# Six layers of local attention and feed-forward: feed-forward loads spread over the queue, inverse roots refined on GpSimd, and new orders within a slot

## What is computed

```python
def attn_layer(x, Wqkv, qs, ksc, Wo):            # 16 heads of 64 channels
    q, k, v = jnp.split(x @ Wqkv, 3, -1)         # x is 128 wide, q, k, v 1024 each
    q = l2norm(q) * qs
    k = l2norm(k) * ksc
    q = q * cos * scale + rotate_half(q) * sin * scale
    k = k * cos * inv + rotate_half(k) * sin * inv
    out = local_attention(q, k, v)               # windows of 32 that see 64 keys
    return out @ Wo
def ffn_layer(x, g, bln, W1, b1, W2, b2):
    xn = (x - mu) / jnp.sqrt(var + 1e-05) * g + bln
    a, gate = jnp.split(xn @ W1 + b1, 2, -1)     # 341 each
    return a * jax.nn.gelu(gate, approximate=False) @ W2 + b2
for i in range(6):
    x = attn_layer(shift_tokens(x), ...) + x
    x = ffn_layer(shift_tokens(x), ...) + x
```

## Time and profile before

| | us |
|---|---|
| median of 3 runs | 3313.07 |
| range of them | 3311.14 to 3315.81 |
| time of the profiled execution | 3313.3 |
| its span | 3311.3 |
| mean granted clock of PE, as a share of 2.4 GHz | 0.977 |

### The profile page before, as it was taken

One profiled execution on the slowest core, in us unless ns is written; L12 is line 12 of the kernel. 1 busy time (PEld: TensorE's weight loads), 2 busy tenths in 40 slices (PEclk: granted clock), 3 DMA queues, 4 the chain that ended last, 5 costly groups with the idle time before them and its releaser, 6 DMA issues.

```text
span 3311.3 us, 181592 instructions
## 1 busy us (share of the span) xinstructions
PE 3127.5 (94%) x71268; PEld 2192.9 (66%) x71268; DVE 2909.5 (88%) x6045; ACT 2666.0 (81%) x5440; POOL 2449.6 (74%) x2672
## 2 busy tenths in 40 slices
PE   6777899999999999999999999999999999999997
PEld 4443567676676767667676677777677776667665
DVE  7886789999899999899999899999899999899995
ACT  6886678888788888788888788888788888788884
POOL 3333678787788878778787787878788887788883
PEclk9887899999999999999999999999999999999997
DMA  2000112122221212212122222222221222212122
GB/s 78 8 7 9 47 51 59 50 59 70 63 59 50 59 50 80 63 51 58 51 58 71 66 55 53 56 53 83 57 56 53 56 53 82 59 51 58 51 53 55
DMA packets 150136, 182.22 MB, mean 55 GB/s; under 512 B 51334, under 2 KB 73924, under 8 KB 149316
## 3 DMA queue, kind: packets, MB, share of 16 engines
q1 hardware_dynamic: 150084, 181.53, 20.5%
HBM read 21.32 MB, written 2.10 MB: 7 GB/s over the span
## 4 chain that ended last, share of the span: by engine, by line
PE 84%; DVE 5%; issue 5%; ACT 2%; DMA 1%; POOL 1%; SPq 1%; DVEq 0%; ACTq 0%; POOLq 0%
PE bank L1221 20%; PE bank L1332 10%; PE bank L1231 9%; PE bank L1308 9%; PE bank L1291 7%; PE bank L1259 7%; PE bank L1361 4%; PE bank L1239 4%; PE bank L1320 4%; PE bank L1369 4%; PE bank L1283 2%; PE bank L1352 2%; PE bank L1346 1%; DMA zm<-zm 1%; DVE XP L833 1%
## 5 line engine op out<-in xcount | busy, mean ns | idle before, releaser
L493 POOL TENSOR_TENSOR qk<-ta,tb 128x512 f32<-128x512 f32 x768 | 971.5, 1276 | 3.7 <-DVE tb L935 3.7
L1221 PE MATMUL bank<-wqkv,zsT 128*128 128x512 f32 x1536 | 821.6, 617 | 13.0 <-ACT vt L674 10.3
L502 POOL TENSOR_TENSOR qk<-qk,rn 128x512 f32<-128x512 f32 x768 | 778.0, 1045 | 4.8 <-DVE rn L954 4.8
L932 DVE TENSOR_TENSOR ta<-bank,rot 128x512 f32<-128x512 f32 x768 | 526.7, 686 | 69.7 <-ACT sq L657 34.5
L935 DVE TENSOR_TENSOR tb<-bank,rot 128x512 f32<-128x512 f32 x768 | 522.2, 680 | 0.0
L533 POOL TENSOR_TENSOR P<-P,rowsum 128x512 f32<-128x512 f32 x384 | 393.0, 1045 | 154.3 <-DVE rowsum L1052 154.3
L657 ACT ACTIVATE sq<-bank 128x512 f32<-128x512 f32 x768 | 465.1, 606 | 14.9 <-PE bank L1221 12.7
L1037 DVE TENSOR_REDUCE bank<-sq 128x32 f32<-128x2048 f32 x192 | 440.6, 2295 | 25.1
L508 POOL TENSOR_TENSOR rstd<-ve,half_neg 128x1 f32<-128x1 f32 x192 | 105.8, 551 | 474.8 <-DVE ve L992 474.8
L665 ACT ACTIVATE qkT<-bank 128x512 f32<-128x512 f32 x768 | 396.6, 602 | 63.0 <-PE bank L1259 63.0
L712 ACT ACTIVATE znT<-bank,gb 128x128 f32<-128x128 f32 x192 | 87.8, 458 | 445.4 <-PE bank L1352 445.4
(11 more groups left out here) (130 smaller groups left out, 5750.4 us busy)
## 6 DMA issues: line engine op xcount, KB each, us to landing
vs<-vt SPq DMA_DIRECT2D x1152, 128.0 KB, 2.4
wqkv<-L_ffn_Wqkv SPq DMA_DIRECT2D x6, 1024.0 KB, 5.1
zm<-zm SPq DMA_DIRECT2D x192, 31.8 KB
wqkv<-L_ffn_Wqkv SPq DMA_DIRECT2D x6, 512.0 KB, 3.8
wo<-L_ffn_Wo SPq DMA_DIRECT2D x6, 512.0 KB, 4.0
z_sb<-x SPq DMA_DIRECT2D x4, 512.0 KB, 5.7
ctxb<-ctx SPq DMA_DIRECT2D x32, 64.0 KB, 1.8
w<-L_ffn_W SPq DMA_DIRECT2D x6, 341.0 KB, 3.0
```

The lines of the kernel that those rows point to most:

```text
L493: g.tensor_tensor(o, i0, i1, ALU.add).then_inc(s["g_add"], 1)
L502: g.tensor_tensor(q3, q3, r3, ALU.mult).then_inc(s["g_qk"], 1)
L932: v_.tensor_tensor(ta[:, c].rearrange("p (h d) -> p h d", d=DH), bank[j % 2][:, :].rearrange("p (h d) -> p h d", d=DH), rot[:, o:o + 64].u ...
L1221: t_.matmul(bank[j % 2][:, :], zsT[:, pu, :], wqkv[:, 512 * j:512 * j + 512], start=True, stop=True).then_inc(s["p_qk"], 1)
```

## The change

Six things change. (1) `load_ffn` is split. The layers' g, b and b1 are loaded once at the start into small_all, and each layer copies its own 128x8 numbers into the tile small with one DMA inside the chip; W1, W2 (now 2 DMAs), b2 and this copy are spread over SP's list around the last and first shifts of two layers. (2) The clamped sums of squares go to a buffer ssq in SBUF, and the refining of the inverse root moves from VectorE to GpSimd, as four instructions of 128x32 (`refine`); the factor 0.5 goes into the rotation tables. (3) The sums of exponentials go to a buffer esum in SBUF. (4) With that, `transpose_qk` waits for d_clamp in place of d_rn and no more for d_rec. (5) PE does `proj_qk(3)` ahead of `transpose_P`, and `ffn_a` ahead of `proj_qk(0)`. (6) VectorE, ScalarE and GpSimd get new orders within the slot.

```diff
+            def load_small(layer):
+                wait(sp, "a_gelu", B * layer)
+                wait(sp, "d_h", B * layer)
+                sp.wait_ge(s["l_small"], 128)
+                sp.dma_start(small[:, :], small_all[:, layer, :]).then_inc(s["l_gb"], 16)
...
+                        sp.dma_start(small_all[0:m, :, 2 + 3 * h + c:3 + 3 * h + c],
+                                     b1[:, h * FF + o:h * FF + o + m].rearrange("l (p o) -> p l o", o=1),
...
             load_o(0)
-            load_ffn(0)
+            load_b2(0)
+            load_w1(0)
+            load_w2(0)
+            load_all_small()
+            load_small(0)
             for b in range(2, B):
                 sp.wait_ge(s["x_A1"], b - 1)
...
+                shift_z(start, 0)
+                if layer > 0:
+                    load_small(layer)
+                    load_w2(layer)
+                shift_v(start + 3, 1)
...
                 if layer + 1 < DEPTH:
+                    load_b2(layer + 1)
                     shift_v(end + 2, 0)
-                    load_ffn(layer + 1)
+                    load_w1(layer + 1)
...
+                def refine():
+                    if m_on:
+                        y = rn[:, pm, :]
+                        wait(pool, "a_rn", count(1, m, 1))
+                        wait(pool, "d_clamp", count(1, m, 1))
+                        g.tensor_tensor(nr[:, 0, :], ssq[:, pm, :], y, ALU.mult).then_inc(s["g_nr"], 1)
+                        wait(pool, "g_nr", count(3, m, 1))
+                        g.tensor_tensor(nr[:, 1, :], nr[:, 0, :], y, ALU.mult).then_inc(s["g_nr"], 1)
+                        wait(pool, "g_nr", count(3, m, 2))
+                        g.tensor_tensor(nr[:, 2, :], three[:, :], nr[:, 1, :], ALU.subtract).then_inc(s["g_nr"], 1)
+                        wait(pool, "g_nr", count(3, m, 3))
+                        g.tensor_tensor(y, nr[:, 2, :], y, ALU.mult).then_inc(s["g_rn"], 1)
...
@@ VectorE's slot @@
                 sum_squares()
-                root(0)
+                clamp()
                 gated()
                 sum_rows()
-                root(1)
+                invert()
                 z_mid()
-                root(2)
-                invert()
-                root(3)
                 rotary(0)
+                rotary(1)
                 z_out()
-                rotary(1)
+                rotary(2)
                 norm_stats()
                 norm_aggr()
-                rotary(2)
                 norm_var()
                 rotary(3)
...
@@ ScalarE's slot @@
+                copy_v(1)
+                square(0)
                 log_sum()
-                copy_v(1)
+                square(1)
                 inverse_root()
-                square(0)
-                if d_on and not (isinstance(n, int) and n - 3 >= UNITS):
-                    act.preload_act_table_set("gelu_and_others")
-                square(1)
                 copy_T(0)
                 copy_T(1)
                 copy_T(2)
+                square(2)
                 copy_T(3)
-                square(2)
+                square(3)
                 copy_PT(0)
-                square(3)
                 copy_PT(1)
                 copy_z()
+                if d_on and not (isinstance(n, int) and n - 3 >= UNITS):
+                    act.preload_act_table_set("gelu_and_others")
                 copy_zn()
...
@@ transpose_qk on PE @@
-                        wait(pe, "d_rn", count(1, m, 1))
+                        wait(pe, "d_clamp", count(1, m, 1))
                         wait(pe, "d_sub", count(2, b - 1, 2))
-                        wait(pe, "d_rec", count(1, b - 1, 1))
```

More of the change, by code:

```diff
@@ L106, in build @@
         w2 = sb("w2", [128, 3, E])
-        gb = sb("gb", [128, 2])
-        b1c = sb("b1c", [128, 6])
+        small_all = sb("small_all", [128, DEPTH, 8])
+        small = sb("small", [128, 8])
         b2r = sb("b2r", [128, E])
@@ L121, in build @@
         rn = sb("rn", [128, 2, 2 * HEADS])
+        ssq = sb("ssq", [128, 2, 2 * HEADS])
+        nr = sb("nr", [128, 3, 2 * HEADS])
+        three = sb("three", [128, 2 * HEADS])
+        esum = sb("esum", [128, HEADS])
         half_neg = sb("half_neg", [128, 2 * HEADS])
@@ L305, in load_o, with load_all_small @@
                 sp.dma_start(wo[:, :, :], Wo[layer, :, :].rearrange("(i p) n -> p i n", p=128)).then_inc(s["l_wo"], 16)
[L307 to L311, removed]
+            def load_all_small():
+                sp.wait_ge(s["u_small"], 1)
                 for o, src in ((0, lng), (1, lnb)):
-                    sp.dma_start(gb[:, o:o + 1], src[layer, :].rearrange("(p o) -> p o", o=1)).then_inc(s["l_gb"], 16)
+                    sp.dma_start(small_all[:, :, o:o + 1], src.rearrange("l (p o) -> p l o", o=1),
+                                 allow_slow_non_contiguous=True).then_inc(s["l_small"], 16)
@@ new lines, in load_w1, with load_w2, load_b2 @@
+            def load_w1(layer):
+                wait(sp, "p_a", B * layer)
+                sp.dma_start(w1[:, :], W1[layer, :, :]).then_inc(s["l_w1"], 16)
+            def load_w2(layer):
+                wait(sp, "p_y2", B * layer)
+                sp.dma_start(w2[:, 0:2, :], W2[layer, 0:256, :].rearrange("(c p) n -> p c n", p=128))\
+                    .then_inc(s["l_w2"], 16)
+                sp.dma_start(w2[0:FF - 256, 2, :], W2[layer, 256:FF, :]).then_inc(s["l_w2"], 16)
+            def load_b2(layer):
+                wait(sp, "g_zmb", B * layer)
@@ L538, in slot @@
                 add(3)
+                residual()
+                add(0)
+                refine()
                 norm_rstd()
+                add(1)
+                next_input()
                 normalize(0)
                 normalize(1)
+                add(2)
                 normalize(2)
                 normalize(3)
[L544 to L548, removed]
             slots(pool, slot, xslot)
@@ L1034, in sum_squares, with clamp @@
                         wait(dve, "a_sq", count(4, m, 4))
-                        wait(dve, "d_rn", count(1, m - 1, 1))
+                        wait(dve, "d_clamp", count(1, m - 1, 1))
                         wait(dve, "d_sub", count(2, c, 2))
-                        v_.tensor_reduce(sm, sq[:, :].rearrange("p (h d) -> p h d", d=DH), AX.X, ALU.add)\
+                        v_.tensor_reduce(SC[0][:, 0:32], sq[:, :].rearrange("p (h d) -> p h d", d=DH), AX.X, ALU.add)\
                             .then_inc(s["d_sumsq"], 1)
+                def clamp():
+                    if m_on:
+                        wait(dve, "d_sumsq", count(1, m, 1))
+                        wait(dve, "g_rn", count(1, m - 2, 1))
+                        v_.tensor_scalar(ssq[:, pm, :], SC[0][:, 0:32], NORM_MIN2, None, ALU.max)\
+                            .then_inc(s["d_clamp"], 1)
                 def sum_rows():
@@ L1378, in slot @@
                 proj_qk(2)
+                proj_qk(3)
                 transpose_P()
-                proj_qk(3)
                 scores()
@@ L1386, in slot @@
                 proj_v(1)
+                ffn_a()
                 proj_qk(0)
-                ffn_a()
             slots(pe, slot, xslot)
```

65 lines of the change are left out of this document (25 added, 40 removed).

## The result

The changed kernel takes 3338.0 us in the median (3336.68 to 3339.28, 4 runs), the kernel before 3312.11 on the same chip (3309.21 to 3315.81). The ratio is 1.008, with a 95% interval from 1.0068 to 1.0092. The forecast was 3268, in 3226 to 3318.

What follows compares the result with a forecast made beforehand. It took PE's steady slot of 15.066 us plus five layer changes as the cost, with the GpSimd lap setting the new slot at 14.96. Sum: 3313.3 - 31.7 - 20 + 6 = 3267.6, so 3268 us, range 3226 to 3318.

Steps and rivals of the forecast that it cites:

- Layer changes: At five layer changes, 6.3 us each, the shift of zm leaves when ready and PE doesn't stand: -31.7 us, at least -16.
- The second lap: Round through GpSimd's sums, refine and rstd, then VectorE's zn to the next sum_rows: 14.96 us, setting the slot, saving 20 us.
- the 0.27 where I had called myself wrong: Sign for GpSimd's 128x32 refining instructions, taken as 0.31 us each: mean below 0.27 or above 0.35 refutes it.
- the first lap: Round from PE's transposes of q and k through copies, square, rotation, norm and zn back to PE: 14.85 us.
- The rival that made GpSimd the bound and the kernel slower: Refining instructions on GpSimd over 0.38 us eat the layer changes' gain: 3335 us at 0.40, 3382 at 0.462; chance 0.13.
- PE's own pace: PE's work per slot falls from 15.07 to about 14.65 us; as rival, slot 14.72, time 3221 us, chance 0.15.
- the likeliest lap to be missing: An unwritten lap holding up proj_qk(3) on PE, which now needs rotary(1) 0.9 us sooner; would make the forecast wrong altogether.
- The start: Eight small loads at kernel start delay the third context tile: +6 us, between nothing and 10 us.
- The Trainium skill's ratio of 1.96: GpSimd sum at 1.96 times VectorE's time: 0.37 us per refining instruction, lap 15.20, time 3313, no change; chance 0.08.

Runs made afterwards that it cites:

- split_only: The kernel before with only the feed-forward loads split and spread over SP's list, orders and refining as before: 3310.2 us, ratio 1.0002.
- split_b2_after: split_only with b2's load moved behind the next layer's first shift of zm, with the copy into small: 3280.6 us, ratio 0.9898.
- rstd_old_pe: rstd_first with P's transposes again between proj_qk(2) and proj_qk(3) on PE: 3274.1 us, ratio 0.989, slot 15.06 us.
- old_pe: The changed kernel with P's transposes again between proj_qk(2) and proj_qk(3) on PE: 3334.4 us, ratio 1.0073, slot 15.39 us.
- small_late: rstd_first with the eight small loads behind the twelfth context tile's load and the copy into small behind the twentieth's: 3257.1 us, ratio 0.9828.
- add_halved: The changed kernel with add(1) on GpSimd done as two instructions of half the size: 3255.7 us, ratio 0.9842, slot 14.94 us.
- rstd_first: The changed kernel with the power for rstd ahead of the four refining instructions on GpSimd: 3255.4 us, ratio 0.9841, slot 14.94 us.
- refine3: The changed kernel without the third of the four refining instructions on GpSimd: 3285.0 us, ratio 0.9922, slot 15.10 us.
- input_first: The changed kernel with the copy next_input ahead of add(1) on GpSimd: 3375.2 us, ratio 1.0198, slot 15.62 us.
- pad_end: The changed kernel with a useless 128x512 sum at the end of GpSimd's slot, behind normalize(3): 3335.1 us, ratio 1.0077, slot 15.37 us.

## Why the prediction was wrong, step by step

- **Layer changes, -31.7 us.** Right in size: they cost nothing now, and the clock stays at 1.00. Incomplete in its reason. I named W1's DMA as all that is left ahead of the shift, and did not see that b2's wait for `residual` stands ahead of it too. With `residual` last on GpSimd the wait stayed (split_only), and with b2 behind the shift it went (split_b2_after); in the changed kernel it is `residual`'s earlier place that lets b2 go out in time.
- **The second lap, 14.96 us.** This is the step that failed. The lap was the right one, and its GpSimd part came out shorter than forecast: `refine` took 1.20 us, not 1.41, since an instruction of 128x32 takes 0.253 us and not 0.31, which is below the 0.27 where I had called myself wrong. But from the end of rstd's power on I charged 0.04 us and then VectorE's path from zn's start (6.45), with zn's 0.61 of before inside. Measured are 1.27 for `add(1)`, 0.09 and 5.74, 7.10 in place of 6.49. That is 0.61 us more, and with the terms that were too large (0.21 for `refine`, 0.08 for the others) it makes 15.28 for the slot shown. The 0.19 more in every other slot, a step that I hadn't seen either, brings the mean to 15.37. I had taken zn's 0.61 for its own length, but it takes 0.35 with GpSimd idle, and the rest was a wait for `normalize`. The hint was in the trace before: `z_mid` and `z_out` take 0.28 us for as many numbers, zn took twice that, and it ended 0.08 us behind a GpSimd instruction. The same 0.61 stands in the first lap.
- **The rival that made GpSimd the bound and the kernel slower** came true in its sign and not in its cause. It needed a refining instruction of over 0.38 us; they took 0.253. That its 3335 for an instruction of 0.40 us lies near the 3338 measured is luck. Its place in the round was right, and what it lacked was `add(1)`.
- **PE's own pace, 14.65.** Not reached by any kernel here. I had read the 0.86 us of two other projections as what the pair would take; it took 2.19 us for the two, as long as apart. The new order still saved 0.12 us a slot and not 0.26 (rstd_old_pe), by a way that no run shows, and only after zn was out of the way. At the end of the prediction I had called the earlier need for `rotary(1)` the likeliest lap to be missing; it takes the pair's gain away, but it isn't what made the kernel slower (old_pe).
- **The start, +6 us.** 3.7 in the profiled execution. The wait for the third context tile comes from the cause named (small_late). But over the ten traces with these loads at the start the first slot begins between 302.8 and 306.9, at 304.5 in the mean, where before it was 302.9. So they cost 1.6 us in the mean, an estimate from single traces, and 3.7 is partly chance.
- **The Trainium skill's ratio of 1.96** for a sum on GpSimd (GPSIMD Engine Reference, section "Elementwise — side-by-side cycle accounting") would make 0.37 us of each refining instruction, an estimate from VectorE's 0.19. Measured are 0.253, a ratio of 1.3. The page's ratio is for N=2048; for 32 numbers the measurement decides.
- **The sum.** Forecast were -31.7 - 20 + 6, so -45.7. Measured are, by the spans of the two profiled executions, -31.7 for the changes of layer, +53.8 for 174 steady slots, +3.7 for the start, +0.9 for the 16 slots ahead of the steady part and -1.7 for what is behind it: +25.0, and 3313.3 + 25.0 = 3338.3. Nearly all of the difference is the slot: 0.309 us more in place of 0.106 less.

What the traces show of zn fits one rule: it ends 0.34 to 0.35 us behind its start, or 0.08 to 0.09 us behind the GpSimd instruction that was there first, whichever is later. So only the last 0.08 us of its time lie behind the other's end.

zn's wait has a rule in the Trainium skill, "SBUF — State Buffer", section "Who interferes with whom": an instruction with one tensor and scalars as inputs, as zn is, may run in a mode that takes the port pair that VectorE shares with GpSimd, whoever comes first holds it for its whole instruction, and the other blocks. The traces agree, with zn's end 79 to 89 ns behind that of a GpSimd instruction in all 150 slots of each of six (before, changed, add_halved, rstd_first, refine3, input_first), and with the GpSimd instruction as the one that is held in the four slots of rstd_first above. Who comes first can't be read from the starts to better than about 0.05 us: in rstd_first's other slots zn starts 0.04 us ahead and is the one held, by 0.03. That it is this mode and this port, and not another thing that the two share, no run here shows: none changed zn's own form.

## What to carry to other kernels

Where two engines can lock each other out, an instruction's mean duration in a profile holds its wait; compare it with its like of the same size, and see which instruction of the other engine ends just before it does. When you reorder an engine's list, look at what now stands beside such an instruction: a long one there became part of the round here, and one of 1.04 us where GpSimd waited anyway was free (pad_end). When loads move in a queue, write down for each what it waits for, since in split_only a wait at the wrong place cost as much as the transfers that it replaced.

## What I had not expected of the hardware

A GpSimd sum or product on 128x32 takes about as long as the copy of 128x2: 0.252 to 0.254 us in the changed kernel's four groups, against the 0.246 of the earlier trace rows.

```profile
L539 POOL TENSOR_TENSOR nr<-ssq,rn 128x32 f32<-128x32 f32 x192 | 48.8, 254 | 0.0
L541 POOL TENSOR_TENSOR nr<-nr,rn 128x32 f32<-128x32 f32 x192 | 48.5, 253 | 15.0
```

The price of a blocked instruction hangs on tenths of a microsecond: with `add(1)` starting 0.15 us ahead of zn in the slot shown of input_first, and at the same time within 0.02 us in others, the slot is 15.62 us; with a short instruction there it is 14.94.
